# Joins and the causal zeroing of an attention moved to GpSimd in a two-layer AdaLN block

## The chip, the cores and the metric

The kernel runs on one core of a Trainium2 chip as one program. The metric is the device time of one execution in microseconds; lower is better. Five engines work side by side: TensorE (PE), VectorE (DVE), ScalarE (ACT), GpSimd (POOL) and SyncE (SP), which issues all transfers here. They meet only through semaphores.

## The reference, cut to what matters

The input is x, 8 batches of 256 tokens with 128 features. Two layers follow, each made of a mixer and a mixture of experts, all with modulated layer norms. The change lies in the mixer of layer 0, a causal attention with 16 heads of 8 features whose keys and values come from a latent:

```python
q = (x @ Wq + bq).reshape(B, T, H, D)
kv_latent = gelu(x @ Wkd + bkd)
lat = kv_latent[..., :L] + kv_latent[..., L:]
kv = lat @ Wku + bku
k, v = kv[..., :C], kv[..., C:]          # both reshaped to B, T, H, D
attn = einsum('bqhd,bkhd->bhqk', q, k) * scale
attn = where(causal, attn, -inf)
attn = softmax(attn, axis=-1)
out = einsum('bhqk,bkhd->bqhd', attn, v).reshape(B, T, C)
return out @ Wo + bo
```

Then come a mixture of 9 experts (8 routed, 1 shared), a gated linear recurrence with an MLP, and a second mixture of 8 experts. The change touches none of them, though one of its edits moves work of the first mixture on GpSimd's queue.

## The kernel before, in words

Everything is kept transposed: 128 features on the partitions, 2048 tokens along the free dimension, in four blocks of 512. The attention runs in 32 units, one for each batch and group of four heads. A head has 32 partitions of its own. Of these, three rows of eight hold parts of the queries (or keys): the value rounded to fp32r and what the rounding leaves, with signs, so that one matmul with rounded operands gives the product at high precision; two more rows carry the negative row maximum against a one.

A unit n goes through these steps, and the engines' programs, written out by hand, interleave several units. The order on each engine is fixed by its `step(n)`:

- PE `project(n)` (L1127, L1128): queries and keys of the unit into bank 6. ACT `evac_proj` (L405 to L409): adds the biases into QT and KT, then writes signed, rounded copies QR and KR. DVE `join` (L728, L730): QX = QT times a mask plus QR, KX likewise. Four units' QX and KX are kept in a ring.
- PE `scores(n, h)` (L1148, L1149): the scores of two heads at a time into banks 0 and 1, queries on the partitions. The second half waits until DVE has read the first (`max_done`), since the two banks are the same. DVE `maxima(n, h)` (L741): adds the causal mask MQ and takes the negative maximum of each row, four instructions a half.
- DVE `spread_max` (L750, L754, L755): rounds the eight maxima into NMH (the tiny cast), copies them to MP, and writes the rest beside them. PE `maxima_t` (L1202): transposes MP. DVE `with_max` (L762): adds them to QX, giving QM.
- PE `scores_t(n, h)` (L1162, L1163): the scores again, keys on the partitions, with the maximum already taken off. Two matmuls per half of the identity with the mask MKK (L1166) add -1e30 above the diagonal. ACT `exps` (L416): the exponential of half a unit in one instruction, into PR, a ring of two units.
- PE `values` (L1178, L1181): the probabilities times the values and ones. ACT `evac_out` (L423); DVE `spread_sum` (L768), ACT `recip` (L428, L430) and DVE `divide` (L776) normalise.

In one round of the loop PE does scores(n+1, 1), scores_t(n, 0), scores_t(n, 1), project(n+3), maxima_t(n+1), scores(n+2, 0), values(n-1). DVE does maxima(n+1, 1), spread_max(n+1), divide(n-3), spread_sum(n-2), with_max(n+1), maxima(n+2, 0), join(n+3). ACT does evac_out(n-2), exps(n), evac_proj(n+3), recip(n-2). The last four units have an output projection (L1193) and `attended` (L789, L792) in place of project and join. PE has filler matmuls at the start (`keep_clock`, L1225).

GpSimd has nothing in the attention. Before it, it makes the constants with memsets and affine selects (L253 makes a mask of 128x128), splits the weights of layer 1 (L267, L269) and the first expert's weights (`split_weights`, L274 and L277) into a rounded part and a rest. After it, it splits normed activations (L285) and weights and, in the mixtures, subtracts (L321) and accumulates (L297). DVE L600 is the modulation of the first norm, L662 and L665 are steps of the router, L875 and L687 belong to the mixture of experts. SP waits for the first expert's split before it loads the second expert's weights.

Of the kernel before, what the change touches and what calls it, by code (L numbers as in the profile page):

```python
# [32 lines left out]
def build(nc, xT, wmod, vecs, mats, kmats, rows, b2, w0, w1, comb0, comb1, outT):  # L33
# [3 lines left out]
    with ctx:  # L37
# [6 lines left out]
        def f(ap):  # L44
            return ap.bitcast(f32)
# [35 lines left out]
        MKK = sb("MKK", [128, 128], bf16)  # L81
# [6 lines left out]
        def mat(name, i=0, n=128):  # L88
# [11 lines left out]
        QX = RA[:, 0:1024].rearrange("p (g n) -> p g n", g=4)  # L100
        KX = RA[:, 1024:2048].rearrange("p (g n) -> p g n", g=4)
        QM = RA[:, 2048:2560].rearrange("p (r n) -> p r n", r=2)
        QR = RA[:, 2560:2816]
        KR = RA[:, 2816:3072]
        NMH = RA[:, 3072:3080]
        MASKED_S = STAT[:, 0:1024].rearrange("p (q j n) -> p q j n", q=2, j=2)
        QT = sb("QT", [128, 256])
        KT = sb("KT", [128, 256])
        NM = sb("NM", [128, 8])
        MP = sb("MP", [128, 2, 128])  # L110
# [34 lines left out]
        (proj_done, qk_evac, qx_ready, s_done, max_done, nmh_done, mp_ready, mt_done, qm_ready, st_done,  # L145
         exp_done, pv_done, ot_done, su_done, ls_done, rsx_done, on_done, vx_ready, wo_done) = map(
            sem, ("proj_done", "qk_evac", "qx_ready", "s_done", "max_done", "nmh_done", "mp_ready",
                  "mt_done", "qm_ready", "st_done", "exp_done", "pv_done", "ot_done", "su_done",
                  "ls_done", "rsx_done", "on_done", "vx_ready", "wo_done"))
        l1_split = sem("l1_split")  # L150
        bias_done = sem("bias_done")
# [89 lines left out]
        def _(gp):  # L241
# [4 lines left out]
            for m in (IDF, IDB, MQ, MKK, MP):  # L246
                gp.memset(m[:], 0.0).then_inc(ident_done, 1)
            gp.wait_ge(ident_done, 5)
            for m in (IDF, IDB):
# [5 lines left out]
            gp.affine_select(out=MKK[:, :], in_=MKK[:, :], compare_op=ALU.is_ge, fill=MASKED, base=0,  # L255
                             pattern=[[1, 128]], channel_multiplier=-1).then_inc(ident_done, 1)
# [57 lines left out]

            gp.wait_ge(moe[0]["w_in"], 16)
# [34 lines left out]
        def _(act):  # L350
# [49 lines left out]
            def evac_proj(n, g):  # L400

                act.wait_ge(proj_done, n + 1)
# [183 lines left out]
        def _(dve):  # L586
# [102 lines left out]

            for t in range(NBLK):  # L690
                centre(0, t)
# [31 lines left out]
            def join(n, g):  # L723

                dve.wait_ge(qk_evac, 4 * n + 4)
                if not isinstance(n, int) or n >= 4:
                    dve.wait_ge(st_done, 2 * n - 6)
                dve.scalar_tensor_tensor(out=QX[:, g, :], in0=QT[:, :], scalar=vec("q_keep"), in1=f(QR),  # L728
                                         op0=ALU.mult, op1=ALU.add).then_inc(qx_ready, 1)
                dve.scalar_tensor_tensor(out=KX[:, g, :], in0=KT[:, :], scalar=vec("k_keep"), in1=f(KR),  # L730
                                         op0=ALU.mult, op1=ALU.add).then_inc(qx_ready, 1)

# [61 lines left out]
            def step(n0, it=0):  # L794
# [15 lines left out]
                if n0 + 3 < UNITS:  # L810
                    join(n + 3, (n0 + 3) % 4)
                else:
                    attended(n0 - 29)

            dve.wait_ge(sp_done, 3)
# [4 lines left out]
            dve.wait_ge(ident_done, 9)  # L820
            dve.wait_ge(in_rows, 32)
            join(0, 0)
# [6 lines left out]
            join(1, 1)  # L829
# [6 lines left out]
            join(2, 2)  # L836
# [211 lines left out]
        def _(pe):  # L1048
# [103 lines left out]
            def scores_t(n, n0, h):  # L1152
# [6 lines left out]
                for j in range(2):  # L1159
                    r = slice(64 * h + 32 * j, 64 * h + 32 * j + 32)  # L1160
                    bank = 2 + 2 * h + j
                    pe.matmul(PS[:, bank, 0:256], KX[r, g, 0:128], QM[r, n0 % 2, :], start=True, stop=False)  # L1162
                    pe.matmul(PS[:, bank, 256:384], KX[r, g, 128:256], QM[r, n0 % 2, 128:256],  # L1163
                              start=False, stop=False)
# [32 lines left out]
            def maxima_t(n, n0):  # L1197
# [3 lines left out]
                for q in range(2):  # L1201
                    mm = pe.transpose(PS[:, 7, 256 + 128 * q:384 + 128 * q], MP[:, q, :], IDF[:, :])  # L1202
# [33 lines left out]
            pe.wait_ge(ident_done, 9)  # L1236
# [326 lines left out]
```

## Time and profile before

| what | value |
|---|---|
| timed runs | 788.62, 786.89, 724.57 us (median 786.89) |
| the profiled execution | 727.6 us, of which the span is 725.8 us |
| PE busy over the span | 631.4 us (87%) |
| DVE | 579.9 us (80%) |
| ACT | 477.5 us (66%) |
| POOL | 200.9 us (28%) |
| chain that ended last | PE 52%, DVE 25%, issue 11%, ACT 10% |

### The profile page before, as it was taken

The numbers are of one execution on the slowest core, as the hardware profiler recorded it, in microseconds if no ns is written. First come the engines' busy times: TensorE is split into PE (matmuls) and PEld (weight loads), VectorE is DVE, ScalarE is ACT, GpSimd is POOL, SyncE is SP. The second block draws the span as 40 slices with busy tenths as digits, with TensorE's granted clock in tenths as the row PEclk, the third lists the DMA queues.
The fourth block names the chain that finished last, engine by engine and source line by source line (L and its number), as shares of the span: only waits on it lengthen the run. The fifth ranks groups of instructions, "written<-read, shape, count | busy, mean of one in ns | idle before, by whom it ended". The sixth has DMA issues, their size and how long they took to land.

```text
span 725.8 us, 11354 instructions
## 1 busy us (share of the span) xinstructions
PE 631.4 (87%) x3252; PEld 435.9 (60%) x3252; DVE 579.9 (80%) x1400; ACT 477.5 (66%) x843; POOL 200.9 (28%) x160
## 2 busy tenths in 40 slices
PE   8689899999997899999999995755997988999983
PEld 5355555555545578888888883332665855666762
DVE  2669999999866668888888977649897788888887
ACT  5438888888644579999999994594452534444441
POOL 3400000000002315455435434201422133444423
PEclk9679999999996999999999999785997999999996
DMA  6000000000000212102222100000000321111111
GB/s 224 30 0 2 2 2 0 0 0 0 1 1 0 89 61 88 61 28 87 87 88 87 59 21 0 23 0 0 1 0 4 139 80 65 72 58 60 66 59 58
DMA packets 6796, 30.88 MB, mean 43 GB/s; under 512 B 906, under 2 KB 1043, under 8 KB 4435
## 3 DMA queue, kind: packets, MB, share of 16 engines
q1 hardware_dynamic: 6756, 30.42, 11.6%
q8 instruction: 17, 0.28, 0.2%
q14 instruction: 23, 0.19, 0.1%
HBM read 29.23 MB, written 1.19 MB: 42 GB/s over the span
## 4 chain that ended last, share of the span: by engine, by line
PE 52%; DVE 25%; issue 11%; ACT 10%; DVEq 1%; DMA 1%; POOL 0%; ACTq 0%; SPq 0%
PE PS L1051 10%; PE PS L1053 10%; PE PS L1052 10%; DVE AR L1021 6%; DVE STAT L741 5%; ACT RA L576 4%; PE PS L1166 2%; PE PS L1064 2%; PE PS L1128 2%; DVE HN L600 2%; PE PS L1193 2%; PE PS L1148 2%; PE PS L1073 2%; PE PS L1162 2%; PE PS L1127 1%
## 5 line engine op out<-in xcount | busy, mean ns | idle before, releaser
L297 POOL TENSOR_TENSOR AR<-AR 128x512 f32<-128x512 f32 x68 | 100.9, 1483 | 228.2 <-DVE AR L687 227.6
L875 DVE TENSOR_TENSOR RA<-AR,RA 128x512 fp32r<-128x512 f32 x140 | 135.3, 992 | 29.7 <-ACT RA L481 28.8
L480 ACT ACTIVATE AR<-PS,BI 128x512 f32<-128x512 f32 x144 | 99.5, 691 | 23.9 <-PE PS L1053 14.0
L1051 PE MATMUL PS<-HH,WH 128*128 128x512 f32 x272 | 108.8, 400 | 1.5 <-DVE AR L1021 1.5
L1052 PE MATMUL PS<-HH,WL 128*128 128x512 f32 x272 | 107.8, 396 | 0.0
L1053 PE MATMUL PS<-HL,WH 128*128 128x512 f32 x272 | 107.7, 396 | 0.0
L1051 PE MATMUL PS<-RA,WH 128*128 128x512 f32 x208 | 86.9, 418 | 17.9 <-DVE RA L1028 17.2
L576 ACT ACTIVATE RA<-AR 128x512 fp32r<-128x512 f32 x64 | 40.5, 633 | 89.9 <-DVE AR L1021 89.9
L481 ACT ACTIVATE RA<-PS,BI 128x512 fp32r<-128x512 f32 x144 | 98.4, 684 | 0.0
L1028 DVE TENSOR_TENSOR RA<-AR,RA 128x512 fp32r<-128x512 f32 x64 | 72.2, 1128 | 27.6 <-ACT RA L576 24.7
L1053 PE MATMUL PS<-RA,WH 128*128 128x512 f32 x208 | 82.2, 395 | 0.0
L1052 PE MATMUL PS<-RA,WL 128*128 128x512 f32 x208 | 82.1, 395 | 0.0
L741 DVE CUSTOM_DVE_ANT_0 STAT<-PS,MQ 128x128 f32<-128x128 f32 (+1 forms) x256 | 76.0, 352 | 1.6 <-PE PS L1149 1.2
L285 POOL TENSOR_SCALAR HH<-HN 128x512 fp32r<-128x512 f32 x8 | 7.7, 959 | 210.8 <-DVE HN L600 210.8
L1051 PEld LDWEIGHTS PS<-RA,WH 128*128 128x128 f32 x208 | 39.5, 190 | 40.3 <-DVE RA L1028 28.6
L1051 PEld LDWEIGHTS PS<-HH,WH 128*128 128x128 f32 x272 | 52.1, 192 | 18.7 <-ACT RA L481 3.0
L1053 PEld LDWEIGHTS PS<-HL,WH 128*128 128x128 f32 x272 | 52.0, 191 | 11.4
L1052 PEld LDWEIGHTS PS<-HH,WL 128*128 128x128 f32 x272 | 52.1, 192 | 9.6
L416 ACT ACTIVATE AR<-PS 128x768 f32<-128x768 f32 x64 | 48.4, 808 | 13.2 <-PE PS L1166 11.5
L1073 PE MATMUL PS<-STAT,OND 128*128 128x512 f32 x48 | 31.2, 757 | 21.9 <-ACT STAT L361 21.9
L687 DVE TENSOR_TENSOR AR<-PS,AR 128x512 f32<-128x512 f32 x68 | 46.0, 680 | 0.9 <-POOL AR L297 0.9
L1053 PEld LDWEIGHTS PS<-RA,WH 128*128 128x128 f32 x208 | 39.6, 190 | 8.7
(183 smaller groups left out, 1197.7 us busy)
## 6 DMA issues: line engine op xcount, KB each, us to landing
AR<-comb SPq DMA_DIRECT2D x17, 1024.0 KB, 4.6
WS<-in_w SPq DMA_DIRECT2D x9, 512.0 KB, 5.5
WS<-in_w SPq DMA_DIRECT2D x8, 384.0 KB, 4.9
M<-in_mats SPq DMA_DIRECT2D x1, 1384.0 KB, 12.1
X<-in_xT SPq DMA_DIRECT2D x4, 256.0 KB, 4.4
out_xT<-X SPq DMA_DIRECT2D x4, 256.0 KB, 2.1
AR<-in_wmod SPq DMA_DIRECT2D x1, 768.0 KB, 9.0
KM<-in_kmats SPq DMA_DIRECT2D x1, 160.0 KB, 9.5
```

The source lines that it names most:

```text
L297: gp.tensor_tensor(out=blk(ACC, t), in0=blk(ACC, t), in1=YW[:, t % 2, :], op=ALU.add)\
L416: act.activation(PR[:, n0 % 2, 2 * h:2 * h + 2, :], PS[:, 2 + 2 * h:4 + 2 * h, 0:384], ACT.Exp, scale=SCALE).then_inc(exp_done, 1)
L480: act.activation(G[:, c, :], PS[:, c, :], ACT.Gelu_apprx_tanh, bias=bias).then_inc(s["act"], 1)
L481: act.activation(GH[:, m0 % 2, c, :], PS[:, c, :], ACT.Gelu_apprx_tanh, bias=bias)\
L576: act.activation(GH[:, m0 % 2, c, :], G[:, c, :], ACT.Copy).then_inc(s1["gh"], 1)
L687: dve.tensor_tensor(out=YW[:, m0 % 2, :], in0=PS[:, 4 + m0 % 4, :], in1=WB[:, slot, t * BLK:(t + 1) * BLK], op=ALU.mult).then_inc(s["ymul" ...
L741: mm = dve.tensor_tensor_reduce(out=MASKED_S[:, q, j, 0:width], in0=PS[:, j, first:first + width], in1=MQ[:, 256 - width:256], scale=-1.0, ...
L875: dve.tensor_tensor(out=GL[:, m0 % 2, c, :], in0=G[:, c, :], in1=f(GH[:, m0 % 2, c, :]), op=ALU.subtract).then_inc(s["lo"], 1)
L1028: dve.tensor_tensor(out=GL[:, m0 % 2, c, :], in0=G[:, c, :], in1=f(GH[:, m0 % 2, c, :]), op=ALU.subtract).then_inc(s1["lo"], 1)
L1051: pe.matmul(out, wh, xh, start=first, stop=False)
L1052: pe.matmul(out, wl, xh, start=False, stop=False)
L1053: return pe.matmul(out, wh, xl, start=False, stop=last)
```

## The change: what it does

ACT's four evacuations all read the projection's bank: QKT is the bank times the keep mask plus a kept bias, QKR the bank times the sign plus a signed bias. The eight columns of biases (KEPT, SIGNED) are made by four small DVE instructions before the attention. GpSimd adds QKT and QKR for queries and keys in one instruction of 128x512. The causal mask of scores_t is dropped; instead GpSimd zeroes the probabilities above the diagonal after the exponential, in four affine selects a unit, each over two heads' 128x128 blocks, and PE's `values` waits for it. The cast to NMH goes: the copy into MP rounds itself, and the rest is taken from there, after a wait. GpSimd's splits for the first expert now come behind all its attention work in its queue.

```diff
-        MKK = sb("MKK", [128, 128], bf16)
...
-        NMH = RA[:, 3072:3080]
+        QKX = RA[:, 0:2048].rearrange("p (g k n) -> p g k n", g=4, k=2)
+        QX, KX = QKX[:, :, 0, :], QKX[:, :, 1, :]
+        QKR = RA[:, 2560:3072].rearrange("p (k n) -> p k n", k=2)
+        QKT = sb("QKT", [128, 2, 256])
+        KEPT = sb("KEPT", [128, 2, 4])
+        SIGNED = sb("SIGNED", [128, 2, 4])
-        MP = sb("MP", [128, 2, 128])
+        MP = sb("MP", [128, 2, 128], r32)
...
+            def causal(n, n0):
+                for h in range(2):
+                    gp.wait_ge(exp_done, 2 * n + h + 1)
+                    own = PR[:, n0 % 2, 2 * h:2 * h + 2, :]
+                    for first in (0, 256):
+                        p = own[:, :, first:first + 128]
+                        ins = gp.affine_select(out=p, in_=p, compare_op=ALU.is_ge, fill=none, base=0,
+                                               pattern=[[0, 2], [1, 128]], channel_multiplier=-1)
+                    ins.then_inc(causal_done, 1)
+
+            def join(n):
+                gp.wait_ge(qk_evac, 4 * n + 4)
+                if n >= 4:
+                    gp.wait_ge(st_done, 2 * n - 6)
+                gp.tensor_tensor(out=QKX[:, n % 4, :, :], in0=QKT[:, :, :], in1=f(QKR), op=ALU.add)\
+                  .then_inc(qx_ready, 2)
+
+            none = gp.to_reg(0.0)
+            for n in range(3):
+                join(n)
+            for n in range(UNITS):
+                causal(n, n)
+                if n + 3 < UNITS:
+                    join(n + 3)
             gp.wait_ge(moe[0]["w_in"], 16)
             split_weights(0, 0, 0, 1024)
...
-                act.activation(QT[:, :], PS[:, 6, 0:256], ACT.Identity, bias=vec("bq", g)).then_inc(qk_evac, 1)
-                act.activation(KT[:, :], PS[:, 6, 256:512], ACT.Identity, bias=vec("bk", g)).then_inc(qk_evac, 1)
-                act.wait_ge(qk_evac, 4 * n + 2)
-                act.activation(QR, QT[:, :], ACT.Copy, scale=vec("q_sign")).then_inc(qk_evac, 1)
-                act.activation(KR, KT[:, :], ACT.Copy, scale=vec("k_sign")).then_inc(qk_evac, 1)
+                for i, name in enumerate(("q", "k")):
+                    act.activation(QKT[:, i, :], PS[:, 6, 256 * i:256 * i + 256], ACT.Identity,
+                                   bias=KEPT[:, i, g:g + 1], scale=vec(name + "_keep")).then_inc(qk_evac, 1)
+                    act.activation(QKR[:, i, :], PS[:, 6, 256 * i:256 * i + 256], ACT.Identity,
+                                   bias=SIGNED[:, i, g:g + 1], scale=vec(name + "_sign")).then_inc(qk_evac, 1)
...
-            def join(n, g):                                    # on DVE: two instructions of 128x256
...
                 dve.wait_ge(max_done, 4 * n + 4)
-                dve.tensor_copy(NMH, NM[:, :]).then_inc(nmh_done, 1)
-                dve.wait_ge(nmh_done, n + 1)
                 if n0 >= 1:
                     dve.wait_ge(mt_done, n)
-                dve.tensor_copy(MP[:, :, 24::32], f(NMH).rearrange("p (q j) -> p q j", q=2)).then_inc(mp_ready, 1)
-                dve.tensor_tensor(out=MP[:, :, 25::32], in0=nmv, in1=f(NMH).rearrange("p (q j) -> p q j", q=2),
+                dve.tensor_copy(MP[:, :, 24::32], nmv).then_inc(mp_ready, 1)
+                dve.wait_ge(mp_ready, 2 * n + 1)
+                dve.tensor_tensor(out=f(MP[:, :, 25::32]), in0=nmv, in1=f(MP[:, :, 24::32]),
                                   op=ALU.subtract).then_inc(mp_ready, 1)
...
-                for j in range(2):
-                    mm = pe.matmul(diagonal(2 + 2 * h + j), IDB[:, :], mask(MKK), start=False, stop=True)
                 mm.then_inc(st_done, 1)
...
             def values(n, n0, it):
-                pe.wait_ge(exp_done, 2 * n + 2)
+                pe.wait_ge(causal_done, 2 * n + 2)
```

## Rows read from the trace of the kernel before

**Rows 1.** Busy us of each engine in a stretch, then clock, DMA share, GB/s.

```profile
120.00:140.00 20.00, 18.01 (x188) 10.61 (x186) 19.62 (x108) 18.05 (x40) 0.00 (x0) 1.00 0.00 0
```

**Rows 2.** Groups of instructions, 60 to 185 us: busy us, mean ns, idle before.

```profile
L741 DVE CUSTOM_DVE_ANT_0 STAT<-PS,MQ 128x256 f32<-128x256 f32 x106 | 40.5, 419 | 0.0
```

**Rows 3.** Chain of waits through one round: start us, us, what.

```profile
149.98 0.33 PE PS L1148 x2
...
151.23 0.32 PE PS L1166 x2
...
151.99 0.63 PE PS L1128 x2
152.61 0.37 PE PS L1202 x2
...
154.71 0.32 PE PS L1148
```

**Rows 4.** Timeline of DVE in the same round: start us, us, instruction.

```profile
150.64 0.28 DVE L741 CUSTOM_DVE_ANT_0 STAT<-PS,MQ 128x128 f32<-128x128 f32 x1
...
151.86 0.17 DVE L750 CAST RA<-NM 128x8 fp32r<-128x8 f32 x1
152.07 0.17 DVE L754 COPY MP<-RA 128x8 f32<-128x8 f32 x1
152.15 0.17 DVE L755 TENSOR_TENSOR MP<-NM,RA 128x8 f32<-128x8 f32 x1
152.23 0.42 DVE L776 TENSOR_TENSOR AR<-OT,SU 128x256 f32<-128x256 f32 x1
...
153.02 0.42 DVE L762 TENSOR_TENSOR RA<-RA,PS 128x256 fp32r<-128x256 f32 x1
153.46 0.29 DVE L741 CUSTOM_DVE_ANT_0 STAT<-PS,MQ 128x128 f32<-128x128 f32 x1
...
154.57 0.48 DVE L728 SCALAR_TENSOR_TENSOR RA<-QT,V,RA 128x256 fp32r<-128x256 f32 x1
```

**Rows 5.** Timeline of ACT in the same round: both exponentials of a unit.

```profile
150.88 1.52 ACT L416 ACTIVATE AR<-PS 128x768 f32<-128x768 f32 x2
```

**Rows 6.** Groups of instructions, POOL, whole span: the affine select of a mask.

```profile
L253 POOL TENSOR_SCALAR_AFFINE_SELECT MQ<-MQ 128x128 f32<-128x128 f32 x1 | 0.3, 296 | 0.0
```

**Rows 7.** Timelines of DVE and POOL in the router and the first mixture.

```profile
234.14 0.29 DVE L662 TENSOR_TENSOR AR<-AR,V 128x128 f32<-128x128 f32 x1
...
235.80 1.27 DVE L665 TENSOR_TENSOR AR<-AR 128x128 f32<-128x128 f32 x1
...
235.57 2.64 POOL L321 TENSOR_TENSOR RA<-AR,RA 128x512 fp32r<-128x512 f32 x2
...
339.40 3.92 DVE L875 TENSOR_TENSOR RA<-AR,RA 128x512 fp32r<-128x512 f32 x2 [0.33 <-ACT RA L481]
...
338.49 1.49 POOL L274 TENSOR_SCALAR WH<-WS 128x1024 fp32r<-128x1024 f32 x1
340.07 2.71 POOL L277 TENSOR_TENSOR WL<-WS,WH 128x1024 fp32r<-128x1024 f32 x1
```

**Rows 8.** Line L687: shortest, median and longest ns, first and last start us.

```profile
L687 DVE TENSOR_TENSOR AR<-PS,AR x68: 673/680/691, 265.1 to 717.9; 128x512 f32<-128x512 f32 x68
```

**Rows 9.** Timelines of DVE and POOL before the attention.

```profile
23.99 2.63 DVE L600 TENSOR_SCALAR HN<-HN,MC,MOD 128x256 f32<-128x256 f32 x2
...
23.30 2.85 POOL L277 TENSOR_TENSOR WL<-WS,WH 128x1024 fp32r<-128x1024 f32 x1
```

**Rows 10.** Chain of waits in the attention's last steps.

```profile
207.47 0.21 DVE X L792
```

**Rows 11.** A stretch at the lower granted clock, columns as in Rows 1.

```profile
40.57:43.98 3.41, 3.41 (x9) 2.28 (x9) 0.92 (x4) 1.75 (x4) 0.00 (x0) 0.50 0.00 0
```

**Rows 12.** Chain of waits at the lower clock, columns as in Rows 3.

```profile
40.58 1.13 PE PS L1128 x2
...
50.55 0.50 PE PS L1166 x2
```

More of the change, by code:

```diff
@@ L144, in build @@
             sem, ("kd_done", "lat_done", "v_psum", "vall_done", "ones_done"))
-        (proj_done, qk_evac, qx_ready, s_done, max_done, nmh_done, mp_ready, mt_done, qm_ready, st_done,
+        (proj_done, qk_evac, qx_ready, s_done, max_done, mp_ready, mt_done, qm_ready, st_done,
          exp_done, pv_done, ot_done, su_done, ls_done, rsx_done, on_done, vx_ready, wo_done) = map(
-            sem, ("proj_done", "qk_evac", "qx_ready", "s_done", "max_done", "nmh_done", "mp_ready",
+            sem, ("proj_done", "qk_evac", "qx_ready", "s_done", "max_done", "mp_ready",
                   "mt_done", "qm_ready", "st_done", "exp_done", "pv_done", "ot_done", "su_done",
@@ L150, in build @@
         l1_split = sem("l1_split")
+        qk_bias = sem("qk_bias")
+        causal_done = sem("causal_done")
         bias_done = sem("bias_done")
@@ L245, in _ @@
             gp.memset(OND[:, :], 1.0 / D).then_inc(const_done, 1)
-            for m in (IDF, IDB, MQ, MKK, MP):
-                gp.memset(m[:], 0.0).then_inc(ident_done, 1)
-            gp.wait_ge(ident_done, 5)
+            for m in (IDF, IDB, MQ, MP):
+                gp.memset(f(m[:]) if m is MP else m[:], 0.0).then_inc(ident_done, 1)
+            gp.wait_ge(ident_done, 4)
             for m in (IDF, IDB):
@@ L254, in _ @@
                              pattern=[[-1, 128]], channel_multiplier=1).then_inc(ident_done, 1)
-            gp.affine_select(out=MKK[:, :], in_=MKK[:, :], compare_op=ALU.is_ge, fill=MASKED, base=0,
-                             pattern=[[1, 128]], channel_multiplier=-1).then_inc(ident_done, 1)
             for b0 in range(2):
@@ L400, in evac_proj @@
             def evac_proj(n, g):
+                if isinstance(n, int) and n == 0:
+                    act.wait_ge(qk_bias, 4)
                 act.wait_ge(proj_done, n + 1)
@@ L688, in moe_scale @@
                                   in1=WB[:, slot, t * BLK:(t + 1) * BLK], op=ALU.mult).then_inc(s["ymul"], 1)
+            dve.wait_ge(in_vec, 16)
             for t in range(NBLK):
@@ L720, in all_values @@
                    .then_inc(vall_done, 1)
-            def join(n, g):
[L725 to L731, printed above, removed]
             nmv = NM[:, :].rearrange("p (q j) -> p q j", q=2)
@@ L809, in step @@
                     maxima(n + 2, n0 + 2, 0)
-                if n0 + 3 < UNITS:
-                    join(n + 3, (n0 + 3) % 4)
-                else:
+                if n0 + 3 >= UNITS:
                     attended(n0 - 29)
+            for i, name in enumerate(("q", "k")):
+                bias = V[:, VAT["b" + name]:VAT["b" + name] + 4]
+                dve.tensor_scalar(KEPT[:, i, :], bias, vec(name + "_keep"), None, ALU.mult).then_inc(qk_bias, 1)
+                dve.tensor_scalar(SIGNED[:, i, :], bias, vec(name + "_sign"), None, ALU.mult).then_inc(qk_bias, 1)
             dve.wait_ge(sp_done, 3)
@@ L819, in _ @@
             dve.tensor_scalar(SP[:, 3:4], SP[:, 3:4], -8.0, None, ALU.mult).then_inc(sp_done, 1)
-            dve.wait_ge(ident_done, 9)
+            dve.wait_ge(ident_done, 7)
             dve.wait_ge(in_rows, 32)
-            join(0, 0)
             all_values(0)
@@ L828, in _ @@
             spread_max(0, 0)
-            join(1, 1)
             with_max(0, 0)
@@ L835, in _ @@
             maxima(1, 1, 0)
-            join(2, 2)
             for n in range(4):
@@ L1162, in scores_t @@
                     pe.matmul(PS[:, bank, 0:256], KX[r, g, 0:128], QM[r, n0 % 2, :], start=True, stop=False)
-                    pe.matmul(PS[:, bank, 256:384], KX[r, g, 128:256], QM[r, n0 % 2, 128:256],
-                              start=False, stop=False)
-                for j in range(2):
-                    mm = pe.matmul(diagonal(2 + 2 * h + j), IDB[:, :], mask(MKK), start=False, stop=True)
+                    mm = pe.matmul(PS[:, bank, 256:384], KX[r, g, 128:256], QM[r, n0 % 2, 128:256],
+                                   start=False, stop=True)
                 mm.then_inc(st_done, 1)
             def values(n, n0, it):
-                pe.wait_ge(exp_done, 2 * n + 2)
+                pe.wait_ge(causal_done, 2 * n + 2)
                 pe.wait_ge(vx_ready, 2 * (2 * it + n0 // 4) + 2)
@@ L1201, in maxima_t @@
                 for q in range(2):
-                    mm = pe.transpose(PS[:, 7, 256 + 128 * q:384 + 128 * q], MP[:, q, :], IDF[:, :])
+                    mm = pe.transpose(PS[:, 7, 256 + 128 * q:384 + 128 * q], f(MP[:, q, :]), IDF[:, :])
                 mm.then_inc(mt_done, 1)
@@ L1235, in _ @@
                     mm.then_inc(v_psum, 1)
-            pe.wait_ge(ident_done, 9)
+            pe.wait_ge(ident_done, 7)
             pe.wait_ge(mod_done, 2)
```

6 lines of the change are left out of this document (removed).

## The prediction

> **What bounds it now.** I read the busy times by stretch first, because POOL's 28% over the span says nothing of the attention. In a stretch of it DVE is busy 19.62 of 20 us, ACT 18.05, PE 18.01, POOL not at all [rows 1]. From 60 to 185 us the wide maximum, four times a unit, appears 106 times [rows 2]: 26.5 units in 125 us, 4.72 us each. Then the chain of waits through one round, from one scores(.,1) to the next, 149.98 to 154.71, 4.73 us [rows 3]. It does not run along the busiest engine: PE works without a gap from 149.98 through the masks, the projection (L1128), the transposes (L1202) and scores(., 0), then DVE takes its four maxima from 153.46, then PE again. Last DVE's timeline [rows 4]: the same 4.73 us without a gap. So two loops are equally long, one through PE and DVE, one of DVE's own work, and shortening one alone gives nothing.
>
> **What each edit takes out.** PE's masks: two entries of 0.32 a round, together 0.65 with the gap behind the first [rows 3]. The PE loop falls to 4.08.
>
> DVE's join: it fills the time from 154.57 to the next maxima at 150.64 + 4.73 = 155.37, 0.80 us [rows 4]. But the next maxima need scores(., 1), which PE starts at 154.71, once the first half is read, and and from PE's start on scores(., 0) at 152.98 (152.61 + 0.37) to DVE's start on them at 153.46 it is 0.48. The result is there at about 155.23, with 0.04 for the matmuls of scores_t that run between. The join was work in the shadow of this round trip, and taking it away leaves DVE idle for nearly all of it: 0.14 gained of 0.80.
>
> The cast: 151.86 to 152.07, 0.21. The rest followed the copy by 0.08; it now has to wait for it, and the cast shows what a dependent pair costs, 0.21. Net 0.08.
>
> With these alone the next limit is DVE with its round trip, 4.73 - 0.14 - 0.08 = 4.51. I check that PE keeps up: the projection ends 0.65 earlier, at 151.97; the maxima are in MP by about 152.11, so the transposes start about 0.2 behind and scores(., 0) end near 153.0, before DVE wants them at 153.24. ACT is busy 18.05 / 20 x 4.73 = 4.27 a round [rows 1] and loses an inner wait, so it stays under 4.51.
>
> **What GpSimd adds.** The join is one 128x512 addition, 1.32 us (half of 2.64 for two) [rows 7]. A select over 128x128 takes 0.296 [rows 6]; over twice the elements it lies between 0.30 and 0.59, and I take 0.49, since part of it is fixed, with starts 0.44 apart. Four selects and a join are 3.3 us, under 4.5, so POOL is no bound by its own work, and the join (from about 153.8, when ACT is done, to 155.2) is ready long before scores(n+3, 0). The values wait for unit n-1, whose exponentials ended a round earlier; that wait is covered. ACT's next evacuation waits for the join; that is covered too, by over 1 us.
>
> What is not covered is that DVE and POOL stand in each other's way. A router step on DVE with both inputs in SBUF takes 0.29 with POOL quiet, and 1.27 when it arrives at 235.80 in a POOL addition (starts 1.3 apart): it ends just behind that POOL instruction [rows 7]. At 339.40 two DVE subtractions take 3.92 us: the first gets through as POOL's split (338.49, 1.49 long) ends, the second stands for the whole next POOL instruction, to 342.78 plus its own work. An instruction with PSUM for one input never suffers: the longest of 68 is 691 ns against a median of 680, POOL or not [rows 8]. So maxima and with_max are safe; the copy, the rest (L755) and divide (L776) have SBUF inputs only.
>
> Their time is just POOL's. The exponentials of a unit start at 150.88 [rows 5]; without masks they start near 150.56 and the first half is done at about 151.37. The selects then run from 151.45, 151.89, 152.33 and 152.77, to 153.25. In the 4.51 round the copy stands at 151.72, the rest at 151.93, divide at 152.01. Walking it through: the copy waits 0.08, to about 151.80; the rest then issues at 152.01, inside the second select, and gets in at 152.24; divide is next at 152.32, and the third select at 152.33. If divide gets in first, with_max moves from 152.80 to 153.11, and the round is 4.51 + 0.31 = 4.82. If it stands until 152.68, with_max moves to 153.47, and the round is 5.18. Both ends hang on 0.01 us, which differs from unit to unit, so I take the middle, 5.00, +0.27 a unit.
>
> The Trainium skill ("SBUF — State Buffer", section "Who interferes with whom") says that a DVE instruction with two SBUF inputs and a GpSimd instruction that reads SBUF exclude each other, and that whichever issues second is blocked until the other has finished. By that rule, the trace agrees: 1.27 against 0.29 and 3.92 for two. It speaks against this change, and read strictly it gives the end at 5.18.
>
> **The ends of the attention.** In the first two rounds and the last three PE alone is the chain (fillers, output projections): 5 x 0.65 = -3.3. The first three joins are on the chain of the start once: 1.32 against 0.80, +0.5. The first expert's splits leave the time before the attention, where DVE L600, from 23.99, stood until POOL's L277 ended at 26.15 [rows 9], on the chain: -1.9 (bounds -2.2 and 0, if the PE work after it were late anyway). They arrive behind the last selects, at about 206; the 2.85 us of L277 then cover 207 to 210, and the addition into X at 207.47, on the chain and with two SBUF inputs [rows 10], stands: +2.0 (0 to 2.5). SP's load of the second expert's weights waits with them, from about 25 to 210 us, and is wanted only near 240. The four bias products take under 0.5 us where DVE waits for ACT: nothing. Sum: -2.7.
>
> **The sum.** 27 x 0.27 = 7.3, less 2.7: +4.6. The profiled execution took 727.6 us (span 725.8 and 1.8 around it), so 732.
>
> **How that stands to the median.** The median of the runs shown is 786.89, 59.3 above the profiled one, and a second run is up there too. 59.3 over 32 units is 1.85 a unit. At the lower clock [rows 11] L1128 takes 1.13 instead of 0.63 and a mask entry 0.50 instead of 0.32 [rows 3, 12], factors 1.79 and 1.56; on PE's 3.48 us of the round these make +1.95 to +2.75. Nearly the same: I take those two runs to be attentions at 1.2 GHz, which no trace here shows. PE would then be the bound, and the change would take 1.0 us of masks from each unit: 4.73 + 1.85 - 1.0 = 5.58, with POOL's blocking hidden behind PE. That is 727.6 + 32 x 0.85 - 2.7 = 752.
>
> **The rivals.**
>
> *No blocking that matters* (the selects hold SBUF for a small part of their time, or start later than the copy). Then the round is 4.51: 27 x -0.22 - 2.7 = -8.6, 719 us. For it: selects are short. Against: both engines' instructions fall in the same 0.6 us by construction, since each follows the same PE work. Chance 0.18.
>
> *Blocking at every step with longer selects* (the slower side). The pattern is two strided rows, priced from a flat one. At 0.59 each, with starts 0.55 apart, the copy waits until 151.95, the rest until 152.5, divide until 153.0: the round is 5.5 and more, 27 x 0.86 - 2.7 = +20.5, 748 us. It decides from a round of 5.37 on. Chance 0.13.
>
> *The clock.* The attention has PE busy 90% now; without masks and with a longer round it is about (4.26 - 0.65) / 5.0 = 72%. If the clock stays at or falls to 1.2 GHz in all executions, it is 752: slower than the profiled run, but faster than the median before by 35 us. For it: two of three runs before lie there. Against: the trace holds 1.00 all through, and the clock was at 0.50 while PE was full [rows 11], so that what came before counts. Chance 0.20, half of it where both kernels are seen at the lower clock.
>
> **How the numbers follow.** The forecast, rounds of 4.82 to 5.18, 727 to 737: chance 0.44. The remaining 0.05 is a gain at the ends larger than mine, with the round at 4.45 (DVE's 3.85 us and the bare round trip). The range runs from 717, under the case without blocking, to 756, over the clock's 752; the likeliest case's own is 724 to 741. A measurement of this kernel tells about 2% from no change, 14.6 us. Slower: 0.13 + 0.10 for the clock + 0.05 of the forecast's tail = 0.28. Faster: 0.10 for both at the lower clock + 0.05 = 0.15. Within 2%: 0.57.
>
> **What would show it.** Right: DVE idle for about 0.6 us before each second maxima, released by L1149's successor; the rest of the maxima or divide stretched from 0.17 and 0.42 to half a microsecond and more, ending just after a select; POOL busy 3 to 3.5 us a unit; L600 at 24 us without its wait and the addition into X near 207 us with one. Wrong: copy, rest and divide at their old durations (then 719); selects over 0.55 us; POOL still working on a join when the next exponential ends; a granted clock of 0.50 between 60 and 190 us.

## The result, and the profile after

The changed kernel takes 758.42, 762.78, 753.67 and 766.17 us (median 760.6). It is slower: its times over those of before are 1.046, 95% interval 1.035 to 1.057. The profiled execution took 758.4 us against 727.6. Executions of before stand at two levels, near 725 us with a mean granted clock of 0.93 to 0.94 and near 787 us with one of 0.82 to 0.83 (the four beside this result are at 788.62, 786.89, 724.57 and 726.66 us); all ratios compare with the first level alone.

The stretches come first, as in [rows 1]: busy us of PE, PEld, DVE, ACT and POOL, then the granted clock.

```profile
43.00:60.00 17.00, 14.03 (x122) 8.30 (x123) 12.88 (x71) 11.24 (x22) 7.76 (x15) 1.00 0.00 1
60.00:80.00 20.00, 20.00 (x128) 10.81 (x122) 13.76 (x77) 15.08 (x30) 10.01 (x18) 0.50 0.01 2
...
120.00:140.00 20.00, 19.47 (x142) 10.68 (x134) 14.01 (x79) 15.79 (x33) 10.61 (x17) 0.62 0.00 0
142.00:162.00 20.00, 19.82 (x130) 10.65 (x130) 13.08 (x75) 14.46 (x30) 9.59 (x16) 0.50 0.00 0
```

The attention starts at the upper clock (1.00, 2.4 GHz) and falls to 0.50 (1.2 GHz) at 60 us, and as long as it stays there PE is busy all the time, where before it had 18.01 of 20 us at 1.00. The clock comes back for 135 to 142 us, is lost again, and returns for good at 224.

The chain of waits through a round at the lower clock, which answers to [rows 3]. L1163 and L1164 are scores, L1177 and L1178 scores_t, L1142 and L1143 project, L1215 maxima_t, L1191 and L1194 values:

```profile
149.82 0.41 PE PS L1163 x2
150.23 0.14 PE PS L1177 x2
...
150.87 1.15 PE PS L1142 x2
152.02 1.15 PE PS L1143 x2
153.17 0.62 PE PS L1215 x2
153.79 0.41 PE PS L1163 x2
154.20 0.32 PE PS L1164 x2
154.52 1.01 PE PS L1191 x8
155.53 0.43 PE PS L1194 x8
155.95 0.41 PE PS L1163 x2
```

From 149.82 to 155.95 it is 6.13 us, all of it PE. At the upper clock the chain has scores(., 1) start at 50.68, 55.18 and 59.68, rounds of 4.50. There DVE's timeline, which answers to [rows 4], reads (start us, us, instruction, idle before):

```profile
55.73 0.29 DVE L758 CUSTOM_DVE_ANT_0 STAT<-PS,MQ 128x128 f32<-128x128 f32 x1 [0.60 <-PE PS L1164]
...
56.97 0.17 DVE L769 CAST MP<-NM 128x8 fp32r<-128x8 f32 x1
57.17 0.29 DVE L771 TENSOR_TENSOR MP<-NM,MP 128x8 f32<-128x8 f32 x1
```

The 4.50 is seen only in rounds that come before the first divide. POOL's timeline of the same round, whose selects answer to [rows 6]:

```profile
54.76 1.28 POOL L329 TENSOR_TENSOR RA<-QKT,RA 128x512 fp32r<-128x512 f32 x1 [1.10 <-issue]
56.67 1.49 POOL L320 TENSOR_SCALAR_AFFINE_SELECT AR<-AR 128x256 f32<-128x256 f32 x4 [0.63 <-ACT AR L442]
```

DVE is idle for 0.60 before the second maxima, the rest (L771) has gone from 0.17 to 0.29, and POOL works 2.8 us a unit. The lines of the rest, the divide (L792) and the selects (L320) over the whole attention, with shortest, median and longest ns:

```profile
L771 DVE TENSOR_TENSOR MP<-NM,MP x32: 175/290/322, 37.1 to 229.7; 128x8 f32<-128x8 f32 x32
L792 DVE TENSOR_TENSOR AR<-OT,SU x32: 410/412/438, 62.0 to 244.5; 128x256 f32<-128x256 f32 x32
L320 POOL TENSOR_SCALAR_AFFINE_SELECT AR<-AR x128: 402/408/675, 47.7 to 235.4; 128x256 f32<-128x256 f32 x128
```

The divide never stands. Where it and a select meet, it is the select that takes longer, 0.67 in place of 0.41, and this happens in nearly every unit. Before the attention, DVE's timeline answers to [rows 9]:

```profile
17.15 3.59 DVE L733 TENSOR_SCALAR GA<-GA 128x32 f32<-128x32 f32 x1
...
21.61 0.73 DVE L626 TENSOR_SCALAR HN<-HN,MC,MOD 128x256 f32<-128x256 f32 x2
```

The modulation (L626) no longer stands behind the first expert's split, but another one (L733) stands behind a split of layer 1. The first scores start at 33.31, where before they started at 36.26. At the end the timeline of DVE answers to [rows 10]; the addition into X takes 1.71 in place of 0.69:

```profile
238.11 1.71 DVE L808 TENSOR_TENSOR X<-X,XC 128x512 f32<-128x512 f32 x1
```

This balances: up to the addition into X the changed kernel needs 238.11 us and before 207.47, a difference of 30.6 of the 30.8 us between the two executions. So the whole loss is in the attention. The second maxima of the first unit start 3.4 earlier (35.64 against 39.02), those of the last unit but one 29.5 later (218.06 against 188.55), and behind them the addition comes 1.1 later still. The 32.9 between the two are made up of 24 full rounds of 6.13 in place of 4.75 (+33.1) and the two rounds in which the clock comes back and goes (+1.1), less 0.7 for three rounds at 4.50 and 0.6 in the first.

### The profile page after: what moved, and what is told of

It is laid out like the page before. It is cut to its first block, busy times and chain, and to the rows that moved or that the text cites. A ratio compares the mean times of both kernels' runs of the same rounds, so it can differ in the third digit from the quotient of the medians.

```text
span 755.6 us, 11146 instructions
## 1 busy us (share of the span) xinstructions
PE 669.2 (89%) x3124; PEld 450.5 (60%) x3124; DVE 561.2 (74%) x1308; ACT 485.8 (64%) x843; POOL 295.3 (39%) x318
## 4 chain that ended last, share of the span: by engine, by line
PE 60%; DVE 18%; issue 11%; ACT 9%; POOL 1%; DVEq 1%; DMA 1%; ACTq 0%; SPq 0%; POOLq 0%
PE PS L1066 10%; PE PS L1067 10%; PE PS L1068 10%; DVE AR L1036 6%; ACT RA L602 4%; PE PS L1142 4%; PE PS L1143 4%; PE PS L1191 3%; PE PS L1163 3%; PE PS L1206 2%; PE PS L1215 2%; PE PS L1079 2%; PE PS L1177 2%; PE PS L1164 1%; PE PS L1194 1%
## 5 line engine op out<-in xcount | busy, mean ns | idle before, releaser
L320 POOL TENSOR_SCALAR_AFFINE_SELECT AR<-AR 128x256 f32<-128x256 f32 x128 | 54.7, 462 | 45.7 <-ACT AR L442 45.7
L329 POOL TENSOR_TENSOR RA<-QKT,RA 128x512 fp32r<-128x512 f32 x32 | 40.8, 1273 | 73.9 <-issue 54.5
L1066 PEld LDWEIGHTS PS<-RA,WH 128*128 128x128 f32 x208 | 39.5, 190 | 41.5 <-DVE RA L1043 28.7
L432 ACT ACTIVATE QKT<-PS,KEPT,V 128x256 f32<-128x256 f32 x64 | 36.2, 566 | 33.2 <-PE PS L1143 33.2
```

Of the source, the lines that this page charges most:

```text
L320: ins = gp.affine_select(out=p, in_=p, compare_op=ALU.is_ge, fill=none, base=0, pattern=[[0, 2], [1, 128]], channel_multiplier=-1)
L1066: pe.matmul(out, wh, xh, start=first, stop=False)
```

## Experiments

"After" is the changed kernel. Each ratio compares with executions of before taken beside it on the same chip, at their lower level near 725 us. A round that holds `place_values`, every fourth one, has two more copies on DVE, from SBUF to SBUF.

**The masks alone, on the kernel before.** TensorE's mask matmuls are left out, and nothing takes their place.

```diff
-                    pe.matmul(... KX[r, g, 128:256], QM[r, n0 % 2, 128:256], start=False, stop=False)
-                for j in range(2):
-                    mm = pe.matmul(diagonal(2 + 2 * h + j), IDB[:, :], mask(MKK), start=False, stop=True)
+                    mm = pe.matmul(... KX[r, g, 128:256], QM[r, n0 % 2, 128:256], start=False, stop=True)
```

> The kernel before with TensorE's mask matmuls of the second scores left out and nothing in their place (the causal mask is missing from the probabilities). CLOCK: the masks alone hold the clock, so it falls to 0.50 early in the attention in most executions, a round takes about 6.1 us (the sum of TensorE's work at the lower clock in the changed kernel, 6.13) and the time is 750 to 770 us. BLOCKING: with the joins on VectorE and nothing on GpSimd nothing is in the way; TensorE's loop is shorter, VectorE's own work of 4.73 us a round bounds, and the time is 722 to 727 us at a clock of 1.00.

Measured: 750.36 to 757.87 us, ratio 1.040 (1.031 to 1.049). Its stretches:

```profile
60.00:80.00 20.00, 20.00 (x118) 10.72 (x118) 15.68 (x88) 14.24 (x29) 0.00 (x0) 0.50 0.01 2
...
120.00:140.00 20.00, 16.84 (x171) 9.98 (x167) 19.55 (x109) 17.75 (x38) 0.00 (x0) 0.95 0.00 0
```

POOL's column is 0.00 and the clock is lost all the same; the rounds at 0.50 are 6.13 to 6.14 us (on its chain scores start at 58.79, 64.93 and 71.06), as in the changed kernel. Removing 0.65 us a round from PE costs 4%: all four executions are at this level.

**The joins, the cast and the biases alone.** The changed kernel without GpSimd's selects and with TensorE's masks back (that part of the edit is shown at the kernel with the masks back, below). The first expert's splits stay behind the attention.

```diff
             for n in range(UNITS):
-                causal(n, n)
                 if n + 3 < UNITS:
                     join(n + 3)
```

> The changed kernel with the causal part undone: masks on TensorE as before, no selects on GpSimd; the join stays on GpSimd and the cast stays gone. CLOCK: as TensorE has all its work, the clock stays at 1.00 in the executions that reach it, and the round is bound by TensorE and VectorE's maxima, 4.73 us as before, less what the transposes gain (0 to 0.2): 718 to 725 us. BLOCKING has one GpSimd instruction a round left, away from the cast and the division: 720 to 730 us. START: near 785 us.

Measured: 718.95 to 725.01 us, ratio 0.9963 (0.9938 to 0.9988), clock 1.00 in all the rounds of the loop:

```profile
80.00:100.00 20.00, 18.23 (x177) 10.75 (x176) 16.78 (x99) 18.54 (x39) 5.64 (x5) 1.00 0.01 2
```

DVE falls from 19.6 to 16.8 busy and the round stays at 4.73 (140.65, 145.40, 150.12), since PE's loop is as long as before: one of two equal loops was shortened. The gain is the start, where the first scores come at 32.18. All ten executions keep the clock with the start of the changed kernel, so the changed start is not what loses it.

**Before with fillers left out**, to see what the upper executions of before are. The three `keep_clock` calls ahead of the loop go.

> The kernel before without the 18 filler matmuls ahead of the attention's rounds. CLOCK: the two executions near 787 us of the kernel before are attentions at 1.2 GHz; without fillers most executions are like them: granted clock 0.50 from 40 to 213 us, a round of 6.6 us, and 780 to 795 us. If the clock comes up by itself in the rounds, the time is at most 724 us, as the fillers' 7.8 us on the chain are gone. The rival holds that the upper executions have another cause; then this kernel is at 717 to 724 us in nearly all executions.

Measured: 793.81 to 796.8 us, ratio 1.097 (1.093 to 1.102), and a stretch of the attention is

```profile
80.00:100.00 20.00, 20.00 (x124) 10.39 (x122) 14.16 (x75) 13.07 (x27) 0.00 (x0) 0.50 0.00 1
```

The same attention at 1.2 GHz takes 69 us more than the median of before beside it (726.92), in rounds of 7.21, where I had expected 6.6. The chain through one:

```profile
145.16 0.41 PE PS L1148 x2
...
145.89 1.01 PE PS L1178 x8
146.90 0.43 PE PS L1181 x8
147.33 0.41 PE PS L1148 x2
...
147.99 0.61 PE PS L1166 x2
...
149.22 0.54 PE PS L1166 x2
149.76 0.85 PE PS L1127 x2
150.61 1.15 PE PS L1128 x2
151.76 0.62 PE PS L1202 x2
152.38 0.41 PE PS L1148 x2
```

7.21 against 6.13: at the lower clock the masks are worth 1.08 us a round. By my estimate an execution of before at 787 is 60 / (7.21 - 4.73) = 24 such rounds, not all 32; no trace shows one. So the change lies between the two levels of before: it is 4.6% slower than the first, and some 26 us faster than the second, where the masks cost more.

**The changed kernel with TensorE's masks back.** The selects stay, on values that are already zero.

```diff
...
-                    mm = pe.matmul(... KX[r, g, 128:256], QM[r, n0 % 2, 128:256], start=False, stop=True)
+                    pe.matmul(... KX[r, g, 128:256], QM[r, n0 % 2, 128:256], start=False, stop=False)
+                for j in range(2):
+                    mm = pe.matmul(diagonal(2 + 2 * h + j), IDB[:, :], mask(MKK), start=False, stop=True)
```

> The changed kernel with TensorE's mask matmuls back beside GpSimd's zeroing (the mask is applied twice, which changes nothing in the output). Theory CLOCK: the changed kernel is slow because without the masks TensorE falls to 1.2 GHz in the attention, where a round takes 6.13 us. With the masks back the granted clock is 1.00 from about 60 us to the end of the attention, a round takes 4.6 to 4.8 us and the time is 722 to 730 us in the executions that keep the clock. Rival BLOCKING: GpSimd and VectorE stand in each other's way, or the values come late; then the masks change nothing and the time stays above 750 us, with the clock high. Rival START: the change of the first microseconds loses the clock, masks or not; then the attention is at 0.50 and the time is near 785 us.

Measured: 785.02, 748.04, 783.51, 785.17 us. That is no cure. The profiled one (785.0) kept 1.00 to about 71 us:

```profile
60.00:80.00 20.00, 18.45 (x158) 10.39 (x151) 14.48 (x83) 15.94 (x33) 10.35 (x16) 0.77 0.01 2
80.00:100.00 20.00, 20.00 (x120) 10.33 (x118) 11.29 (x60) 13.18 (x27) 9.01 (x15) 0.50 0.00 1
```

Its rounds at 1.00 are 4.74 and 4.75, and the last one before the fall 5.13. It is the first that holds `place_values`, whose two copies stood behind selects there (0.80 us in place of 0.43). So a second suspect: POOL's selects delay DVE in that round, PE waits, and the clock goes. But one long round is not enough. Before, without any work on GpSimd, has a round of 5.09 at the same place (its second maxima start at 69.79 and at 74.88) and keeps the clock; PE's timelines, first before, then this kernel, show nearly the same gap in front of the values:

```profile
73.21 0.64 PE L1178 MATMUL PS<-AR 128*32 128x256 f32 x8 [0.63 <-DVE RA L762]
...
69.69 0.64 PE L1196 MATMUL PS<-AR 128*32 128x256 f32 x8 [0.68 <-DVE RA L781]
```

Before itself was at its upper level in 5 of the 13 executions beside it, so four executions alone prove little.

**More matmuls in place of the masks.** Two fp32 matmuls of 128x128 a round in scores_t(., 1), their result unused.

```diff
+                if h == 1:
+                    for _ in range(2):
+                        pe.matmul(PS[:, 5, 384:512], OND[:, :], OND[:, :], start=True, stop=True)
```

> The changed kernel with two filler matmuls a round (128x128 in fp32, into unused columns of bank 5) at the head of scores_t(n, 1), where TensorE's loop has about 0.4 us to spare at the higher clock. CLOCK: if the fillers hold the clock at 1.00, the round is 4.5 to 4.6 us (4.50 was seen in the changed kernel between 50.68 and 59.68 us, at 1.00), with 0.4 us more where values are placed (one round in four, 5.13 against 4.74 in the kernel with both masks and selects): 715 to 724 us. If the clock falls as in the kernel with the masks back, 780 us. BLOCKING by selects in each round: 730 us or more at a clock of 1.00.

Measured: three executions at 731 to 734 us and three at 775 to 776; ratio 1.011 (1.007 to 1.014) for the former. The profiled one held the clock for 50 us longer than after, then lost it:

```profile
60.00:80.00 20.00, 17.99 (x170) 11.24 (x168) 17.01 (x91) 17.70 (x37) 11.78 (x20) 1.00 0.01 2
...
114.00:120.00 6.00, 6.00 (x36) 3.10 (x37) 2.39 (x15) 3.97 (x9) 2.04 (x3) 0.50 0.00 0
```

Rounds at 1.00 are 4.91 to 4.93, and those with `place_values` 5.12 to 5.20, where I had expected 4.5 to 4.6: a miss. The second suspect is alive.

**The same, with the selects out of DVE's way.**

```diff
             def causal(n, n0):
+                if n0 >= 3:
+                    gp.wait_ge(on_done, n - 2)                 # divide(n-3) is done
+                if n0 % 4 == 0 and n0 > 0:
+                    gp.wait_ge(vx_ready, 2 * (n // 4) + 2)     # place_values is done
```

> As the kernel with two fillers a round, and the selects of unit n also wait until VectorE has done divide(n-3) and, every fourth unit, the placing of values. Then no VectorE instruction with SBUF inputs alone meets a select. If the wait of placed values behind selects is what lets the clock fall in the kernel with the masks back, this one holds 1.00 in all executions, with a round of 4.5 us in all rounds: 712 to 720 us. If blocking costs nothing, it equals the kernel with fillers alone. If the later selects delay the join and so the round, it is slower than that by 0.1 us a round or more.

Measured: ten executions, all at 726.54 to 731.23 us, ratio 1.0047 (1.0024 to 1.0071), clock 1.00 to the end and rounds of 4.91 to 4.93 in every unit. I had expected 4.5: a miss, as the two fp32 matmuls take 0.64 us on PE's chain, as long as the masks they stand for. The chain has another 0.2 that it had not before: the first pair of the projection takes 0.63 on it in place of 0.43.

**The late selects alone**, without fillers or masks: the two waits above, on the changed kernel.

> The changed kernel with its selects held until divide(n-3) and the placing of values are done, no fillers, no masks. CLOCK: TensorE still lacks the masks' work, so the clock falls and the time is 750 to 766 us as for the changed kernel. BLOCKING: with the two engines out of each other's way the loss is gone: 716 to 725 us.

Measured: 748.27 and 757.83 us, ratio 1.038 (1.029 to 1.046). The two stretches around the loss:

```profile
70.00:80.00 10.00, 8.40 (x80) 4.59 (x79) 8.59 (x54) 9.94 (x21) 6.06 (x11) 1.00 0.01 2
80.00:90.00 10.00, 9.59 (x73) 5.54 (x73) 6.71 (x40) 7.83 (x18) 5.52 (x10) 0.55 0.01 2
```

Rounds at 1.00 are 4.38 once the waits act (from the fourth unit on), with `place_values` 4.63. The rest is back at 0.17 and no select is over 0.412 us, so the blocking is gone, and the clock falls at 81 us nevertheless. So the missing mask work loses it alone, as it did without GpSimd. The 4.38 is also the true bare round; with every fourth one at 4.63 the mean is 4.45.

**Late selects and cheap fillers.** Four 16-bit matmuls of 128x128 a round.

```diff
+                if h == 1:
+                    for _ in range(4):
+                        pe.matmul(PS[:, 5, 384:512], IDB[:, :], IDB[:, :], start=True, stop=True)
```

> The changed kernel with the late selects of e8_late_only, and four more filler matmuls of 128x128 in 16-bit in each unit's step scores_t(.,1), where before had the h=1 masks. It computes the reference. Theory A (TensorE's clock falls because the removed mask matmuls were work that held it; GpSimd's work itself is free): the fillers hold the granted clock at 1.00 from the start of the attention to its end, the rounds stay at the 4.4 (4.6 with place_values) that e8_late_only shows between 60 and 80 us, and the time is that of before less 0.2 to 0.35 a round in 27 rounds and less 3 at the start: 713 to 719. Theory B (the columns of the fillers are too few, or of the wrong kind, to hold it): the clock falls to 0.50 within the attention and the time is near 750. Theory C (the fillers lie on PE's chain as the fp32 ones of e6 did): clock 1.00, round 4.6 to 4.75, 720 to 726.

Measured: 717.49 to 733.19 us, median 720.4, ratio 0.992 (0.990 to 0.995). The clock holds at 1.00; the fillers are on PE's chain for 0.33 and the round is 4.60, with `place_values` 4.63:

```profile
143.87 0.33 PE PS L1167 x2
...
144.41 0.33 PE PS L1180 x4
...
148.47 0.33 PE PS L1167 x2
```

That is theory C's way, at the lower edge of its times. One execution of nine was at 733.2 with a mean clock of 0.917 (the others 0.932 to 0.941).

**All masks back and late selects**, which sets the second suspect against the first experiment on it: the masks' edit and the waits' edit together.

> The changed kernel with all masks back on TensorE (the selects on GpSimd stay, and now find masked values already zero) as e1_masks_back, and the selects held until after the divide of three units before and in every fourth unit until after place_values. In e1 rounds were 4.74 at the full clock until the first round that held place_values took 5.13, and the clock fell then. Theory A (that stall by the shared port lost the clock): here the rounds are 4.74 throughout, the granted clock stays at 1.00 and the time is 720 to 726. Theory B (the selects between the exponential and the values lose it by themselves, by PE's waits before the values): clock 0.50 from about 70 us on, as in e1, 780 to 786.

Measured: ten executions at 721.85 to 725.41 us, ratio 0.998 (0.996 to 1.000); 1.00 throughout, rounds of 4.72 to 4.75 with `place_values` or without. The two waits alone turn 748 to 785 us into 722 to 725. With all the masks there, selects that start as soon as they can are what put the clock at risk. PE's wait for them before the values is not: it is there in both kernels.

**Half the masks.** TensorE masks the heads of h=1, GpSimd zeroes those of h=0, late.

```diff
             def causal(n, n0):
-                for h in range(2):
+                for h in range(1):
...
+                if h == 1:
+                    for j in range(2):
+                        mm = pe.matmul(diagonal(2 + 2 * h + j), IDB[:, :], mask(MKK), start=False, stop=True)
...
-                pe.wait_ge(causal_done, 2 * n + 2)
+                pe.wait_ge(causal_done, n + 1)
+                pe.wait_ge(exp_done, 2 * n + 2)
```

> Half of the masks: TensorE adds the mask for the two heads of h=1 (two matmuls a unit), GpSimd zeroes those of h=0 alone (two selects a unit, with late waits), the join on GpSimd and the cast gone as in the change. It computes the reference. Theory A (clock held by the amount of TensorE's work at hand): two masks a unit are about half of what was taken away; either they hold the clock at 1.00 and the round is bound by VectorE at 4.4 to 4.5, 713 to 719, or they don't, 740 to 755. I put 0.55 on the first. Theory B (any stall of PE by GpSimd's selects costs the clock, whatever the masks): 740 to 760, since the selects of h=0 are still waited for before the values.

Measured: four executions at 712.18, 714.57, 715.75 and 731.6 us, median 715.2, ratio 0.985 (0.977 to 0.993) for the first three, the best of all. Stretch and chain:

```profile
120.00:140.00 20.00, 16.85 (x170) 9.74 (x168) 17.24 (x103) 19.54 (x41) 8.32 (x13) 1.00 0.00 0
```

```profile
141.21 0.33 PE PS L1170 x2
...
145.59 0.33 PE PS L1170 x2
...
149.98 0.33 PE PS L1170 x2
```

Rounds of 4.38, and 4.63 with `place_values`, the bare rounds. The profiled execution holds the clock, and the mean granted clock of two more is as high; the fourth was at 731.6 with 0.898 in place of 0.934 to 0.938, so the edge is near. The mask matmuls that stay lie in PE's slack and cost nothing: the rounds are those of the kernel without masks. ACT is now the fullest engine, 19.54 of 20.

**The same with the selects early.** Only the two waits are taken out of it.

> e10_half with its late waits taken out again: TensorE masks the heads of h=1, GpSimd zeroes those of h=0 as soon as their exponential is done, as in the change. It computes the reference. e10_half ran at a granted clock of 1.00 all through, in rounds of 4.38, at 712 to 717 us. Theory A (the missing mask work loses the clock, GpSimd's place is of little weight): the clock stays at 1.00, rounds 4.4 to 4.6 with 0.2 to 0.4 more in the place_values rounds, 715 to 721. Theory B (the shared port's stretch in the place_values round loses the clock, as it seemed to in e1_masks_back): the clock falls to 0.50 from the first such round on, near 67 us, and the time is 750 to 780.

Measured: ten executions at 726.35 to 744.99 us, median 733.3; the six below 735 have a ratio of 1.0084 (1.0053 to 1.0115). Stretches:

```profile
80.00:90.00 10.00, 8.62 (x76) 4.91 (x76) 7.66 (x46) 8.33 (x17) 4.08 (x6) 0.81 0.01 2
90.00:100.00 10.00, 10.00 (x76) 5.87 (x76) 6.20 (x36) 7.80 (x17) 3.31 (x4) 0.50 0.00 2
```

Rounds begin at 63.09, 67.81, 72.30, 76.80, 81.30 and 86.01 us on its chain: 4.50, and 4.71 to 4.72 with `place_values`. The clock goes in the round after the last of these, comes back at about 107, goes near 124, comes back near 151 and goes near 168, the last two times near the end of the third round after one with `place_values`. Neither theory holds: no lasting loss as in B, no hold as in A, and no single round can be named as the cause. Against the half masks with late selects this prices the blocking at a steady clock: 4.50 - 4.38 = 0.12 in an ordinary round and 4.71 - 4.63 = 0.08 in one with `place_values`, whose copies keep their 0.21 each here.

**The first expert's splits alone**, on the kernel before: they are held until the last exponential.

```diff
+            gp.wait_ge(exp_done, 2 * UNITS)
             gp.wait_ge(moe[0]["w_in"], 16)
             split_weights(0, 0, 0, 1024)
```

> The kernel before with GpSimd's splits of the first expert's weights (L274, L277) held until the last exponential of the attention. By the prediction's terms, 1.9 us are gained before the attention, where L600 stood behind L277, and 0 to 2.5 are lost behind it: 724 to 727 us in executions at the higher clock, beside 724 to 727 of the kernel before. If the whole lead of about 3 us that the changed kernel has at its first scores comes from the splits, and the loss behind is 1.1 us (1.71 against 0.69 for the addition into X), it is 722 to 725 us.

Measured: ten executions at 718.87 to 723.51 us, ratio 0.994 (0.992 to 0.996), most of them below both of the expected ranges. The first scores start at 33.26, 3.0 earlier, and the splits run clear of the addition into X:

```profile
199.91 1.04 POOL L274 TENSOR_SCALAR WH<-WS 128x1024 fp32r<-128x1024 f32 x1 [178.66 <-ACT AR L417]
201.04 2.35 POOL L277 TENSOR_TENSOR WL<-WS,WH 128x1024 fp32r<-128x1024 f32 x1
```

Of the 19 executions of before beside it 4 were at the upper level and none of these ten.

## Why the prediction was wrong

The step that failed is the term that the forecast put at nothing: what the missing mask matmuls do to TensorE's clock. The sum took a round of 5.00 at a granted clock of 1.00 and came to 732 us, and the fall of the clock stood as a rival with a chance of 0.20. The runs showed the fall in its place, in every execution (mean granted clock 0.822 to 0.844), and in the profiled one 24 full rounds of 6.13 at 0.50. The rival's own sum, 752, was too low as well.

- **Two equal loops of 4.73** [rows 1 to 4]: right. The joins and the cast off DVE alone leave 4.73. PE's loop without the masks is longer than the 4.08 of the sum, by the 0.2 of the projection (4.60 - 0.33 and 4.91 - 0.64 are 4.27), but it still does not bound.
- **The bare round, 4.51**: 4.38 measured, and 4.63 where `place_values` adds two copies, which the prediction did not walk through; the mean of 4.45 is near. In the shadow of the join DVE does wait, 0.60 where the sum had 0.66. That the changed kernel ran at 4.50 was a coincidence of two misses, 4.38 bare and 0.12 of blocking.
- **Blocking, +0.49 an ordinary round, taken between 0.31 and 0.67**: 0.12 measured. A select takes 0.41 and not 0.49 (four take 1.49, with starts 0.36 apart). The rest is stretched to 0.29 in nearly all units, the copy seldom (0.41 at 139.76), and the divide, on which both ends of the sum hung, in none: it gets in first, and the select stands. The Trainium skill ("SBUF — State Buffer", section "Who interferes with whom") has the mechanism, in which the later one of the two waits. With the later one read as DVE's each time it gave 5.18, and the runs show 4.50.
- **The ends**: L600 free at 21.61: right, and the first scores are 2.95 us earlier (1.9 less 0.5 was the estimate; the splits alone, moved on the kernel before, give 3.0, beyond the bound of 2.2). The addition into X stands 1.0, not 2.0.
- **The clock's price**: mis-sized in "4.73 + 1.85 - 1.0 = 5.58". The 59.3 us were spread over 32 units, where by my estimate some 24 rounds run at 1.2 GHz, at 2.48 each. The prediction's own scaling of PE's work, +1.95 to +2.75, had the 2.48 within it. The masks' 1.0 was right (1.08). So the round is 6.13 and not 5.58, in 24 rounds and not in 32: +32.9 in place of +27.2, and the rival's total would have been 758 and not 752. That the two errors are of opposite sign is luck. The values, 1.01 + 0.43 us, are on PE's chain at the lower clock alone, where they stand for the 1.25 of DVE's maxima.
- **The clock's chance.** The argument against it was that the trace held 1.00 all through and that what came before the attention decides. The rows that spoke louder were the times: two of three runs near 787 show that this attention is at the edge with all its masks, and an edit that takes 0.65 of 4.26 us of work from the engine whose clock is in question makes it worse. Leaving the masks out does it by itself (1.040). What had no price in the argument was how near to the edge the kernel before is.

Shown: missing masks suffice to lose the clock (ratio 1.040 without any GpSimd work, 1.038 with late selects; with the changed kernel these are ten executions, all at a mean granted clock of 0.822 to 0.854, where before has both levels), and early selects put it at risk of themselves (half masks: ten executions between 726 and 745 against three at 712 to 716 and one at 731.6 with the waits; all masks: four at 748 to 785 against ten at 722 to 725). The change has both. Not shown: how TensorE's recent work is weighed, and what in the early selects costs the clock, since before keeps it through a round as long as theirs; that half the masks are enough here with late selects, and not with early ones, is all the runs say.

## What to carry to other kernels

Where some runs of a kernel are some 8% above the others, find out first whether the clock fell in them: then an edit that takes matmuls off TensorE, or makes it wait a few tenths of a microsecond more a round, is priced at the clock and not at the matmuls. Take off only what the other loop can use: here half of the masks gave all of the gain in the round (4.38), and full removal lost 4%. Such an edit is worth trying by halves, and executions should be counted by level. Work moved to GpSimd should be started, by a wait, in the part of the round where VectorE reads PSUM: here the wait took 0.12 us off a round.

## What the runs showed of the hardware

- A full PE need not bring the clock back soon: in the changed kernel it stayed at 0.50 from 60 to 135 us with PE busy without a gap (20.00 of 20 from 60 to 80 us), and returned then for 7 us only, under the same loop. The Trainium skill ("TensorE: Matmul & The Clock Gate", section "HAM oscillation — how this bites in real kernels") puts the oscillation of its example down to idle gaps behind transfers. This case is another one: with the late selects alone, PE's timeline just before the loss, which comes at 81.0, has gaps of 0.29 us at most, all behind DVE:

```profile
80.16 0.44 PE L1219 MATMUL PS<-IDF,MP 128*128 128x128 f32 x2 [0.29 <-DVE MP L775]
81.27 1.08 PE L1195 MATMUL PS<-AR 128*32 128x256 f32 x8 [0.25 <-DVE RA L782]
```

- Edits far from the loop go with how often the clock is lost. With the starting fillers left out it was all four executions. With the first expert's splits after the attention it was none of ten, where before was at the upper level in 4 of 19; that alone may be chance. But three more kernels with the late splits (the joins alone, the fp32 fillers and all masks, these two with late selects) have none in thirty, while before was up there in 15 of the 51 executions beside the four.
- A select over 128x256 elements takes GpSimd 0.41 us undisturbed, against 0.296 for half the elements [rows 6], and 0.67 where it meets DVE's divide, which keeps its own 0.41.
